# Two routed layers and their attention: the setup as one row of fifteen units, norm and routing by chunk

## What is computed

```python
def _L0_ffn_ref(x):                    # called twice, with x layer-normed
    xf = layernorm(x) * ln_gamma + ln_beta
    tile_idx = argmax over the 64 tiles, within the best of 8 clusters, of sign(xf) @ tile_sigs.T
    x_slice = xf[8 features of the token's tile]
    mn, mx = per tile, over all 2048 tokens routed to it, min and max of x_slice
    u = clip((x_slice - mn) / (mx - mn + 1e-08), 0.0, 1.0 - 1e-06)
    gi = int(u * 16)
    delta = (bases[tile, j, gi] + slopes[tile, j, gi] * (u * 16 - gi)) * output_scale[tile]
    return x + delta scattered to the 8 features
x = x + 0.5 * _L0_ffn_ref(_layernorm(x), ...)
x = x + _L0_attn_ref(_layernorm(x), ...)    # q, k, v, rotary; sin/cos features of q and k;
                                            # the product with v is taken inside each token
x = x + 0.5 * _L0_ffn_ref(_layernorm(x), ...)
x = x + 0.5 * _L1_ffn_ref(_layernorm(x), ...)   # Hadamard, W_up, W_gate, silu, Hadamard, W_down
x = x + _L1_attn_ref(_layernorm(x), ...)        # causal, two softmaxes
x = x + 0.5 * _L1_ffn_ref(_layernorm(x), ...)
```

## Time and profile before

| | us |
|---|---|
| median of 3 runs (lowest, highest) | 2363.11 (2361.16, 2364.78) |
| the profiled execution, its span | 2363.24, 2361.5 |
| PE, DVE, ACT busy | 2062.1, 1227.2, 746.9 |
| opening, setup row | 0 to 38.4, to 207.4 |
| lead-in, passes −1 to 3 | to 252.35, to 743.0 |
| tail, feed part | to 815.4, to 2361.5 |

### The profile page before, as it was taken

The page is one execution under the profiler, slowest core; times in us unless marked ns, Lnnn a source line. Parts: engine busy times, 40 slices in busy tenths (PEclk is TensorE's granted clock), DMA queues, the critical chain, the costliest instruction groups (busy, mean ns, idle before and its releaser), DMA issues. The chain is left out here.

```text
span 2361.5 us, 29596 instructions
## 1 busy us (share of the span) xinstructions
PE 2062.1 (87%) x12078; PEld 987.3 (42%) x12078; DVE 1227.2 (52%) x2281; ACT 746.9 (32%) x1163; POOL 220.9 (9%) x164
## 2 busy tenths in 40 slices
PE   5885669697975499989999899999998999999998
PEld 3553233334343344434444444444444444444443
DVE  5554364757643455463666265644565356623332
ACT  4562231324341112322235223432244223511211
POOL 3630202120200000000000010001000000000000
PEclk7886769797966599999999999999999999999999
DMA  7224030302021222322111111111111111122321
GB/s 258 83 72 167 1 58 1 58 1 58 8 52 72 81 72 98 110 87 72 45 42 59 53 46 37 63 36 63 54 55 45 54 46 54 63 90 99 116 93 68
DMA packets 90978, 158.75 MB, mean 67 GB/s; under 512 B 44182, under 2 KB 55772, under 8 KB 86108
## 3 DMA queue, kind: packets, MB, share of 16 engines
q1 hardware_dynamic: 90844, 156.86, 20.7%
HBM read 128.52 MB, written 18.87 MB: 62 GB/s over the span
## 5 line engine op out<-in xcount | busy, mean ns | idle before, releaser
L1169 PE MATMUL ps<-arena 128*128 128x512 f16 (+1 forms) x4512 | 1018.3, 381 | 22.6 <-DVE arena L1932 12.9
L1169 PEld LDWEIGHTS ps<-arena 128*128 128x128 f16 x4512 | 436.4, 99 | 542.8 <-issue 48.5
L1877 PE MATMUL ps<-arena 128*128 128x512 f16 x1536 | 349.0, 383 | 29.5 <-DVE arena L1923 16.3
L1877 PEld LDWEIGHTS ps<-arena 128*128 128x128 f16 x1536 | 147.4, 98 | 207.4 <-issue 29.4
L1899 ACT ACTIVATE arena<-ps,arena 128x512 f32<-128x512 f32 x128 | 87.6, 684 | 362.4 <-PE ps L1169 362.1
L1932 DVE SCALAR_TENSOR_TENSOR arena<-arena,ps 128x512 f32<-128x512 f32 x128 | 87.8, 686 | 210.1 <-ACT arena L1899 209.5
L2486 ACT ACTIVATE arena<-ps 128x1024 f32<-128x1024 f32 (+3 forms) x128 | 90.1, 704 | 253.7 <-PE ps L2395 253.6
L2591 DVE CAST arena<-arena 128x1024 f16<-128x1024 f32 (+3 forms) x128 | 66.6, 520 | 149.8 <-ACT arena L2486 147.7
L2557 DVE TENSOR_REDUCE arena<-ps 128x2 f32<-128x256 f32 (+3 forms) x128 | 99.5, 819 | 65.1 <-PE ps L2339 65.1
L1960 DVE SCALAR_TENSOR_TENSOR arena<-ps,arena 128x512 f32<-128x512 f32 x64 | 44.0, 687 | 139.6 <-PE ps L1877 139.4
L1941 DVE SCALAR_TENSOR_TENSOR arena<-ps,arena 128x512 f32<-128x512 f32 x128 | 95.7, 748 | 39.5 <-PE ps L1169 39.3
(11 more groups left out here) (265 smaller groups left out, 2446.7 us busy)
## 6 DMA issues: line engine op xcount, KB each, us to landing
arena<-wug_dram SPq DMA_DIRECT2D x128, 512.0 KB, 3.3
arena<-wd_hi_dram SPq DMA_DIRECT2D x16, 1024.0 KB, 5.0
arena<-wd_lo_dram SPq DMA_DIRECT2D x16, 1024.0 KB, 7.2
arena<-arena SPq DMA_DIRECT2D x144, 64.0 KB, 2.1
wug_dram<-arena SPq DMA_DIRECT2D x4, 2048.0 KB, 15.4
arena<-_attn_hidden_states_dram SPq DMA_DIRECT2D x4, 1024.0 KB, 12.4
arena<-in_L_ffn_W_up_dram SPq DMA_DIRECT2D x8, 512.0 KB, 4.4
arena<-in_L_ffn_W_down_dram SPq DMA_DIRECT2D x4, 1024.0 KB, 7.7
```

The costliest lines, as they stand in the source:

```text
L1169: ins = pe.matmul(out, left[a](c), right[b](c), start=(at == 0), stop=(at == 3 * n - 1))
L1877: ins = pe.matmul(k.ps[:, bank, :], act[x][:, slot, cols], wd[y][:, f, :], start=(f == 0 and m == 0), stop=(f == 7 and m == 2))
```

## The change

The opening's weights and the row become one row of 15 units (WEIGHTS), in which the three units of attention weights stand at places 7, 11 and 14 and are only turned. Its first load is that of the first W_up group. The route of chunk i begins at unit ROUTE_UNIT[i] = 1, 5, 8, 11; the norm is made per chunk (token_sums, token_first, token_second, the functions that the second route used already). The sign is taken straight from PSUM. Mask, its products and slice go: DVE multiplies the normed tokens with the one-hot, broadcast over 8, and reduces over the 64 tiles with a strided read; gamma and beta of the chosen tile come by four small matmuls (gain) and are put on in ends. The stores of the ug weights are issued one unit each along the row. The first chunk's one-hot turn, 256 columns of its rows and its scale stand at the end of the row and only three columns behind minmax; the wait for the biases stands behind the norm's sums. The tail is made likewise.

In the passes, the spline lookup of look moves into the loop over y, in one bank (LOOK_BANK); the sums keep one bank, the tables are one step earlier, value stands ahead of output, the last twelve of the 36 feature DMAs behind the values, and the picks of back run at the pass's end and at y = 1 and 2 of the next. The last chunk's route in pass 3 moves from y = 6 to 13 to y = 8 to 15. In the diff, lines left out are marked.

```diff
-def route_slice_tensor(k, pe, i, n, bank):
-
-    s = k.s
-    gate(pe, s["r_picked"], nth(i, n, KC, 2 + KC), s["gates"])
+def route_gain_tensor(k, pe, i, n, bank):
+
+    s = k.s
+    gate(pe, s["r_oht"], i + n)
     for u in range(TPC):
-        for c in range(KC):
-            ins = pe.matmul(k.ps[:, bank, 256 + u * DSL:256 + (u + 1) * DSL], k.y[:, u, c * P:(c + 1) * P], k.c["lane"],
-                            start=(c == 0), stop=(c == KC - 1))
-    ins.then_inc(s["r_slice"], 1)
+        ins = pe.matmul(k.ps[:, bank, 256 + 2 * DSL * u:256 + 2 * DSL * (u + 1)], k.hot_t[:, u * P:(u + 1) * P],
+                        k.table[:, 260:276], start=True, stop=True)
+    ins.then_inc(s["r_gain"], 1)
...
 def route_sign_scalar(k, e, i, n, c, banks):
     s = k.s
-    gate(e, s["r_turned"], nth(i, n, KC, c + 1), s["gates"])
-    y = feature_block(k.y, c)
-    e.activation(y, token_columns(k.ps[:, banks[c % 2], :]), ACT.Identity, bias=k.beta[:, c:c + 1],
-                 scale=k.gamma[:, c:c + 1]).then_inc(s["r_y"], 1)
-    gate(e, s["r_y"], nth(i, n, KC, c + 1), s["gates"])
-    e.activation(token_columns(k.sgt[:, c, :]), y, ACT.Sign).then_inc(s["r_sign"], 1)
+    if c == 0:
+        need(e, s["routed"], i + n - 1)
+    gate(e, s["r_turned"], nth(i, n, KC, c + 1))
+    e.activation(k.sgt[:, c, :], k.ps[:, banks[c % 2], :], ACT.Sign, bias=k.beta[:, c:c + 1],
+                 scale=k.gamma[:, c:c + 1]).then_inc(s["r_sign"], 1)
...
-def route_pick_vector(k, V, i, n, c, banks):
+def route_pick_vector(k, V, i, n, u):
     s, e = k.s, V.eng
-    gate(e, s["r_mask"], nth(i, n, KC, c + 1), s["gates"])
-    y = feature_block(k.y, c)
-    e.tensor_tensor(y, token_columns(k.ps[:, banks[c % 2], :]), y, ALU.mult).then_inc(s["r_picked"], 1)
+    gate(e, s["r_hot"], i + n)
+    y = k.y[:, u, :]
+    hot = k.onehot[:, bass.ds(i * TPC + u, 1), :].squeeze(1)
+    V.link(e.tensor_tensor(y.rearrange("p (t j) -> p t j", j=DSL), y.rearrange("p (t j) -> p t j", j=DSL),
+                           bcast(hot.unsqueeze(2), [P, NTILE, DSL]), ALU.mult))
+    e.tensor_reduce(k.sliced[:, bass.ds(i * TPC + u, 1), :].squeeze(1), y.rearrange("p (t j) -> p j t", j=DSL), AXX, ALU.add)
...
-    gate(e, s["r_slice"], i + n, s["gates"])
-    cells = k.ps[:, bank, 256:256 + TPC * DSL].rearrange("p (u j) -> p u j", u=TPC)
+    cells = k.sliced[:, bass.ds(i * TPC, TPC), :]
+    V.link(e.tensor_scalar(k.off, hot, 1.0, BIG, ALU.subtract, ALU.mult))
+    gate(e, s["r_gain"], i + n)
+    gain = k.ps[:, bank, 256:256 + 2 * DSL * TPC].rearrange("p (u c) -> p u c", u=TPC)
+    V.link(e.tensor_tensor(cells, cells, gain[:, :, 0:DSL], ALU.mult))
+    e.tensor_tensor(cells, cells, gain[:, :, DSL:2 * DSL], ALU.add).then_inc(s["r_cut"], 1)
+    gate(e, s["r_cut"], i + n + 1)
...
+WEIGHTS = (("ug", 0), ("ug", 1), ("ug", 2), ("down", 0), ("ug", 3), ("ug", 4), ("down", 1), ("w0", 0),
+         ("ug", 5), ("down", 2), ("ug", 6), ("w0", 1), ("down", 3), ("ug", 7), ("w0", 2))
...
+SCALE_DOWN_AT = ((0, 2), (2, 1), (4, 2), (7, 0))
...
+    for n in range(GROUPS):
+        if n in LOADED and LOADED.index(n) + 2 < len(LOADED):
+            load_nat(LOADED.index(n) + 2)
+        if n < 2:
+            load_x(n + 2)
+        if n == 2:
+            load_down(2)
+        if WEIGHTS[n] == ("down", 0):
+            load_down(3)
+        if n:
+            store(n - 1)
     sp.wait_ge(s["routed"], NCH)
...
-ROUTE_AT = {"stats": (0, 1), "turn": ((0, 3), (1, 0), (1, 1), (1, 2)), "sign": ((1, 0), (1, 1), (1, 2), (1, 3)),
-            "key": (2, 0), "hot": (2, 1), "mask": ((2, 2), (2, 2), (2, 3), (2, 3)), "slice": (3, 0), "ends": (3, 1)}
+    return k.wdt[side][part][:, 4 * r:4 * r + 4, :] if kind == "down" else k.wt[side][part][:, :, r * P:(r + 1) * P]
+
+
+ROUTE_UNIT = (1, 5, 8, 11)
+ROUTE_AT = {"sums": (-1, 2), "first": (-1, 3), "second": (0, 0), "write": (0, 1),
+            "turn": ((0, 3), (1, 0), (1, 1), (1, 2)), "sign": ((1, 0), (1, 1), (1, 2), (1, 3)),
...
+            if (n, r) == (GROUPS - 1, 3):
+                apply_turn_tensor(k, pe, 0, 1, READY_BANK)
...
+            if (n, r) == (GROUPS - 1, 1):
+                e.wait_ge(s["wd_mixed"], NCH)
+                spline_start_vector(k, V, 0)
+            if (n, r) == (GROUPS, 2):
+                scale_start_vector(k, V, 0)
+                scale_tiles_vector(k, V, 0, range(TPC))
...
+def ready_cols_tensor(k, pe, ready, banks, parts):
+
+
+    pe.wait_ge(k.s["table_ready"], ready)
+    for u in range(TPC):
+        ins = pe.matmul(k.ps[:, banks[u], 256:259], k.oht[:, u * P:(u + 1) * P], k.table[:, 256:259], start=True, stop=True)
+    ins.then_inc(k.s["ap_rows"], parts)
...
-SUM_BANK = (5, 6)
+SUM_BANK = 5
...
-QK_AT = (1, 2, 4, 5, 7, 8)
-ROT_AT = (3, 4, 6, 7, 9, 10)
-LENGTH_AT = (5, 6, 8, 9, 11, 12)
-SPREAD_AT = 13
-REFINE_AT = 15
+QK_AT = (0, 1, 3, 4, 6, 7)
+ROT_AT = (2, 3, 5, 6, 8, 9)
+LENGTH_AT = (4, 5, 7, 8, 10, 11)
+SPREAD_AT = 12
+REFINE_AT = 14
+LOOK_START, LOOK_PLACE, LOOK_SLOPE, LOOK_VALUE = 3, 6, 8, 11
...
+            if now:
+                pe.wait_ge(s["b_res"], TPC * now)
...
-        if y % 4 == 0 and y >= 8:
-            pe.wait_ge(s["b_ot_lo"], TPC * now + y // 4 - 1)
+        if y % 4 == 0 and y:
+            pe.wait_ge(s["b_ot_lo"], TPC * now + y // 4)
...
+            if y == LOOK_START:
+                look_turn_tensor(k, pe, look)
+            if y in (LOOK_PLACE - 1, LOOK_SLOPE, LOOK_VALUE - 1):
+                look_part_tensor(k, pe, look, (LOOK_PLACE - 1, LOOK_SLOPE, LOOK_VALUE - 1).index(y))
...
+    for z in range(4):
+        turns(z)
+        value(z)
+    turns(4)
     output(0)
-    if look is not None:
-        look_rows_tensor(k, pe, look)
...
-    sp.wait_ge(s["b_f_lo"], 6 * i + 6)
-    spread(k.qs, (0, 1, 0), slice(4, 6), slice(2, 4), s["b_qs"])
...
+    sp.wait_ge(s["b_f_lo"], 6 * i + 6)
+    spread(k.qs, (0, 1, 0), slice(4, 6), slice(2, 4), s["b_qs"])
...
-            sp.wait_ge(s["had_lo"], 4 + 4 * 3 * NCH)
-            for f in range(0, FB, TPC):
-                sp.dma_start(d["wug"][f:f + TPC].rearrange("f p n -> p f n"), k.wug_flat[:, f:f + TPC, :])\
-                    .then_inc(s["ug_out"], 16)
...
             setup_tensor(k, pe)
+            ready_rows_tensor(k, pe, 0, 1, ROWS_BANK)
             minmax_tensor(k, pe, 1, "")
-            use_work(k, k.work, k.h, k.work[:, 2048:4096])
-            pe.wait_ge(s["b_in"], 160)
-            apply_turn_tensor(k, pe, 0, 1, LOOK_CELLS)
-            look_rows_tensor(k, pe, 0)
-            pe.wait_ge(s["ap_read"], 1)
+            ready_cols_tensor(k, pe, 1, ROWS_BANK, 3)
+            pe.wait_ge(s["ap_read"], 3)
             for c in range(KC):
                 turn_tensor(k, pe, 0, c, FIRST_TURN[c])
...
             minmax_vector(k, V, 1, "")
-            use_work(k, k.work, k.h, k.work[:, 2048:4096])
-            V.link(dve.memset(k.acc, -BIG))
+            dve.memset(k.acc, -BIG)
+            spline_place_vector(k, V, 0, 3, side_rows(k)[0])
+            spline_slope_vector(k, V, side_rows(k)[1])
+            spline_value_vector(k, V, side_rows(k)[2])
+            dve.sem_inc(s["ap_read"], 2)
+            add_scatter_vector(k, V)
+            add_sum_vector(k, V, 0)
+            norm_sums_vector(k, V, 0, range(TPC))
+            norm_spread_vector(k, V)
             dve.wait_ge(s["b_in"], 160)
             V.link(dve.tensor_copy(k.spread.rearrange("p (h f) -> p h f", f=32),
                                    bcast(k.c["ident"][0:24, 0:24].unsqueeze(2), [24, 24, 32])))
-            spline_start_vector(k, V, 0)
-            cells, slopes, bases = look_rows(k)
```

713 lines of the change are left out of this document (336 added, 377 removed).

## The result

The changed kernel takes 2344.41 us (median of 4 runs, 2343.41 to 2345.25), the kernel before beside it 2363.86 (2361.16 to 2364.78). The ratio is 0.9922, with a 95% interval of 0.9907 to 0.9937: 19.4 us faster, where 61 were forecast, and outside the range of 2276 to 2330. The sign was right and the size was not.

What follows compares the result with a forecast made beforehand. Outside the unchanged, PE-bound feed part, it saw dependent chains and setup units bound by PE or DVE. Setup −23, lead-in −13.5, passes −10.5 and tail −14 gave −61, so 2363.2 became 2302 us; forecast 2288 to 2316, range 2276 to 2330.

Steps and rivals of the forecast that it cites:

- first and second, some thirteen dependent steps on four columns that I estimate at 0.2, 2.6: Setup row, per chunk: the norm's small dependent DVE steps at 0.2 us each, 2.6 of a chunk's 17.0 us of DVE.
- the forecast 184: Setup row: last mix at 184 us instead of 207.4, −23, between 175 and 196.
- the five units with the choice, picks and ends: Setup row, units 3, 4, 7, 10, 13: bound by DVE, 5.8 us each of their own plus route work, 69.3.
- the seven bound by PE: Setup row, units 1, 2, 5, 6, 9, 11, 14: 8.6 to 10.4 us plus about 1.6 each for cold clock, 75.7.
- the two short ones: Setup row, units 8 and 12, behind attention weights with nothing to mix: 12.9 us together.
- 40 of the route's 68 us: Setup row: share of the four chunks' DVE route work falling in the five DVE-bound units; the rest in units before.
- Rival (a): Setup row: PE idles behind DVE, so the clock falls; row ends at 253, whole kernel takes 2371 us; chance 0.04.
- Rival (b): DVE bounds wherever picks stand and the sum bank stalls three times a pass: +26 us, 2328 us; chance 0.22.
- The lead-in: 44.95 us after the setup row: bias wait, one-hot turn, most row matmuls and scale leave, −13.5 (−9 to −17).
- The tail: 72.4 us after the passes: picks replace slices and masks −5.8, signs −2, rows −3.9, scale −2.5; −14 (−11 to −16).
- The passes: Passes −1 to 3: −1.5, −1.7, −7.8, +1.5, −1; sum −10.5 us, range −28 to +6.
- The price of SP's issues: Pass −1: 36 DMA issues in 30.57 us, 0.85 each; path to first score 39.9 instead of 43.6, −3.7.

Runs made afterwards that it cites:

- the roots in PSUM alone: Changed kernel with seed and root of the chunk's norm in a free PSUM bank, nothing left out: 2318.30 us, ratio 0.9816, row's end 208.2.
- the first experiment: Changed kernel with POOL's Hadamard folding of W_down cut to 8 columns, the folding left out: 2309.84 us, ratio 0.9782, row's end 201.3.
- ScalarE's queue: Roots-in-PSUM kernel with ScalarE's root steps one step later and W_down scalings moved ahead: 2319.88 us against 2318.30.
- a heap of DVE work in few units: Norm of chunks 1 to 3 in units 2, 6, 9: 2307.50 against 2309.84 without POOL's folding; 2311.03 against 2314.77 with quarters, PSUM, two sum banks.
- smaller pieces of the sums: Kernel with quarters, PSUM and two sum banks, moved norm's four statistics one to a step in units 1, 5, 9: 2310.12 us against 2311.03.
- the experiment on the order: Changed kernel with all 36 feature DMAs ahead of the values again, as in the kernel before: 2354.22 us, ratio 0.9959.

## Why the prediction missed

The setup row. The step that failed is the price "first and second, some thirteen dependent steps on four columns that I estimate at 0.2, 2.6", and with it the products at 0.68: it left out the wait for POOL. In the changed kernel the steps took up to 2.28 us, and the holds added 35.7 us to DVE. Undisturbed they are 0.16 to 0.17, so the estimate was good for an idle machine. But it was not asked what runs beside them: the earlier trace rows shows POOL busy 74.7 us of the row and none in the lead-in, and L1136 and L1080, from which the sense of DVE's prices came, lie where POOL is idle. The rows with POOL at work, L985 and L994 in the earlier trace rows, both read PSUM, as do all wide steps of the old row that fall beside POOL; the row's only products with both inputs in SBUF, L559 and L561, fall between POOL's bursts (82.25 and 84.06, with POOL idle from 76.5 to 85.4). The change removed products on PSUM (L543) and brought in products and small steps on SBUF only, and the diff shows that: `ps,arena` became `arena` in the order's rows. It also took away the wait that had kept POOL back until the norm was done.

The kernel before did show the hold, in its passes. The small steps of the second route's norm, the very functions that the change moved, stand there twice beside POOL's shorter instructions, at 479 and 597 us:

```profile
479.04 1.04 POOL L1518 TENSOR_TENSOR arena<-arena 128x512 f32<-128x512 f32 x1 [5.86 <-DVE arena L1584]
479.07 1.03 DVE L388 SCALAR_TENSOR_TENSOR arena<-arena 128x4 f32<-128x4 f32 x1
480.04 1.09 POOL L1515 TENSOR_TENSOR arena<-arena 128x512 f32<-128x512 f32 x1
480.13 1.01 DVE L389 SCALAR_TENSOR_TENSOR arena<-arena 128x4 f32<-128x4 f32 x1
```

The longest instruction of the line, and not its median (0.165 us for L388), would have told it.

The row ended 47.7 us later than the forecast 184. Of these, 30.4 go with POOL's work, 23.5 of them with the roots in PSUM alone. By the prediction's own sign, a setup that ends after 200 makes the frame of its sum wrong.

The other 17 lie in the prices by unit. Without holds the five units with the choice, picks and ends take 75.0 and not 69.3, the seven bound by PE 81.8 and not 75.7, the two short ones 19.2 and not 12.9 (from the ends of the units of the first experiment). The term "40 of the route's 68 us" was right in amount: DVE's route work in the five is 40.1 us. But the prediction let the rest, 27 us, cost nothing in the other units. Of it 7.1 each stand in units 8 and 11 (the fourth pick and the ends of one chunk, the norm's second of the next) and 5.0 in unit 14; DVE is busy 9.9 of 12.0 us in unit 8, where 6.45 was forecast for the whole, and 12.1 of 12.7 in unit 11. Units 1 and 5, 12.8 and 12.9 with DVE busy 7.8, aren't explained so. In the whole row DVE has 134.8 of 188.0 us and PE 131.4, and neither is the bound alone: the picks' 28 us cost 16 to 18.5. How the rest divides is open. Two theories for it, ScalarE's queue and a heap of DVE work in few units, gave nothing or 1 to 5 us of the row, and so did smaller pieces of the sums.

Rival (a), the clock, was wrong: PEclk is 0.84 with PE idle 83 of 218 us. The clock does swing, as the Trainium skill's "TensorE: Matmul & The Clock Gate", section "HAM oscillation — how this bites in real kernels", has it: matmuls behind a stall are cold (3.42 at 25.58 against 1.89) and warm again one step later, as in the earlier trace rows. That the clock would stay down, and 2371, was the prediction's own reading of the rule, and the trace doesn't bear it out. Rival (b), DVE as the bound, was nearest in kind, but put its 26 us on the reduces (0.05 each in fact) and the banks (in passes 2 and 3 nothing to be seen; the waits themselves were longer than the 1.7 given as a sign, up to 3.5).

The lead-in was right, −13.0 for −13.5: the wait for the bias of the earlier trace rows is gone, and the columns' matmuls that stay, as PE's timeline has them, take what was forecast as 1.7:

```profile
236.68 1.69 PE L1024 MATMUL ps<-arena 64*128 64x3 f32 x8 [0.94 <-DVE arena L593]
...
253.76 0.54 DVE L2813 COPY arena<-arena 24x768 f32<-24x768 f32 x1
```

The tail was −11.8 for −14. Choice to minmax, 14.6 us before, takes 10.2 (PE's L476 at 758.36 to L583 at 768.56), not 8.8; the last 0.8 of the 2.2 is open.

The passes gave 7.3 us more than forecast: −6.1, −4.6, −7.2, +2.5 and −2.4 for −1.5, −1.7, −7.8, +1.5 and −1. In pass −1 the loop over y, up to the first feature matmul, grew by 5.6 us (5.9 were worked out for pass 0), and the part behind it shrank by 11.7, not by some 7. The price of SP's issues was mis-sized: in the timeline of its queue they took less than the 0.85 that the earlier trace rows gave:

```profile
323.44 18.42 SPq L1537 DMA_DIRECT2D arena<-arena  x24
...
345.06 4.02 SPq L1553 DMA_DIRECT2D arena<-values_dram  x8
...
349.13 7.63 SPq L1537 DMA_DIRECT2D arena<-arena  x12
```

That is 0.77 and 0.64 us each, and the 24 hold a wait of 2.6; from the first issue to the first score at 358.31 it is 34.9 us, where 39.9 were worked out. Each issue takes 0.64 us from start to start in both kernels. The 36 of the kernel before are 23.0 us of issues and 7.5 of waiting for features in between, so that 30.57 / 36 was no price of an issue. And by the experiment on the order, the order itself gave its gain in passes 1 and 3, not at this boundary, where the prediction put 3.7.

## What to carry to other kernels

Before a small chain of VectorE steps is moved, look at what GpSimd does at the new place, and whether the chain's inputs both lie in SBUF: a 0.16 us step can become as long as the GpSimd instruction beside it. One input from PSUM freed the steps here, and GpSimd's instructions in quarters bounded the hold at 0.7 us. The wait of the kernel before kept the two apart; a wait that seems to be there for no data may be doing just that. When a price is taken from a row, ask which neighbours it had in that row.

## What the runs showed of the hardware

The hold works both ways: of POOL's instructions of 2.35 us those that ran beside a pick's product took 2.75 to 2.89 (2.82 at 68.92). Splitting is not free: 0.76 us for 256 columns, 2.35 for 1024. A reduce with 8 outputs costs no more than one with 32 (0.686 for both), and a stride of 32 bytes 0.39 us more over 512 elements.
